# Where the exponentials of the next unit stand among ScalarE's copies in a multi-head attention loop

## What is computed

```
x = x + L0_xattn(ctx, ctx, layernorm(x))      # 16 heads, softmax((q k^T) / sqrt(128)), out @ W_out.T + b_out
x = x + L0_ffn(layernorm(x))                  # 8 experts, the best 2 weighted, gelu
x = x + L1_xattn(layernorm(x), ctx)           # 1 head
x = x + L1_ffn(layernorm(x))                  # 8 experts and a shared one
x = x + L2_xattn(layernorm(x), ctx)           # 16 heads, two softmaxes: attn1 - lambda * attn2, rms norm, projection
x = x + L2_ffn(layernorm(x))                  # 8 experts with a capacity
x = x + L3_xattn(layernorm(x), ctx)           # 16 heads, rotated q and k, a bias by position, a gate
x = x + L3_ffn(layernorm(x))                  # 8 experts, silu(a) * g
```

```
attn = softmax(q @ k.T * scale, axis=-1)      # 512 x 77 per head and batch
out = attn @ v                                # heads side by side, then a projection to 128
```

## Time and profile before

| | |
|---|---|
| median of 3 runs | 1227.28 us (1226.39 to 1229.32) |
| profiled execution, its own time | 1229.32 us |
| its span | 1227.5 us |
| PE busy | 975.9 us, 79% |
| PEld busy | 824.3 us, 67% |
| DVE busy | 636.9 us, 52% |
| ACT busy | 550.9 us, 45% |
| POOL busy | 398.7 us, 32% |
| mean granted TensorE clock | 0.87 |

### The profile page before, as it was taken

One profiled execution on the slowest core, in us unless ns is written; L12 is line 12 of the kernel. 1 busy time (PEld: TensorE's weight loads), 2 busy tenths in 40 slices (PEclk: granted clock), 3 DMA queues, 4 the chain that ended last, 5 costly groups with the idle time before them and its releaser, 6 DMA issues. The chain is left out here.

```text
span 1227.5 us, 20580 instructions
## 1 busy us (share of the span) xinstructions
PE 975.9 (79%) x7706; PEld 824.3 (67%) x7706; DVE 636.9 (52%) x1741; ACT 550.9 (45%) x1051; POOL 398.7 (32%) x396
## 2 busy tenths in 40 slices
PE   3887999999978999878888742989349876199992
PEld 3565899999957999745666522888226664188882
DVE  7787311111266343668788723344377784444442
ACT  1665444344434334346556421655327543155552
POOL 4443200000013002400010244446555546635551
PEclk9988899999996899979889755999769776589996
DMA  9999900000000000000000003655200000355543
GB/s 336 168 172 167 187 33 2 1 1 1 1 1 1 1 1 1 1 1 2 1 1 2 10 26 114 187 168 176 74 1 1 2 5 27 93 162 183 167 148 103
DMA packets 70577, 83.69 MB, mean 68 GB/s; under 512 B 5297, under 2 KB 57528, under 8 KB 70352
## 3 DMA queue, kind: packets, MB, share of 16 engines
q1 hardware_dynamic: 64336, 71.85, 25.9%
q0 software_dynamic: 4992, 8.45, 2.0%
q10 hardware_dynamic: 1152, 2.10, 0.5%
HBM read 52.02 MB, written 32.18 MB: 69 GB/s over the span
## 5 line engine op out<-in xcount | busy, mean ns | idle before, releaser
L2198 ACT ACTIVATE hT<-PS,par 128x512 f32<-128x512 f32 x200 | 136.8, 688 | 184.3 <-PE PS L2146 182.8
L2238 DVE SCALAR_TENSOR_TENSOR X<-PS,wts,X 128x128 f32<-128x128 f32 x272 | 76.6, 344 | 230.0 <-PE PS L2158 230.0
L822 PE MATMUL PS<-par,score 128*116 128x128 f32 x704 | 117.3, 308 | 18.9 <-ACT score L1035 6.2
L1054 ACT ACTIVATE hT<-PS 116x512 f32<-116x512 f32 (+1 forms) x192 | 102.1, 560 | 56.5 <-PE PS L822 55.2
L2158 PEld LDWEIGHTS PS<-regA,hT 128*128 128x128 f32 x1024 | 119.2, 192 | 2.8
L2158 PE MATMUL PS<-regA,hT 128*128 128x128 f32 x1024 | 119.4, 275 | 0.0
L822 PEld LDWEIGHTS PS<-par,score 128*116 128x116 f32 x704 | 90.4, 153 | 30.3 <-issue 16.3
L1123 POOL TENSOR_TENSOR score<-score,mx 128x1232 f32<-128x1232 f32 x32 | 72.0, 2251 | 101.3 <-DVE mx L931 101.3
L1909 PE MATMUL PS<-q_up,halves 128*112 128x256 f32 (+1 forms) x276 | 88.0, 319 | 15.3 <-DVE hT L2021 8.7
L835 PE MATMUL PS<-hT,vblk 116*32 116x128 f32 x1408 | 85.3, 302 | 10.4 <-DVE oc L951 9.5
L2144 PE MATMUL PS<-x_up,w_halves 128*128 128x512 f32 x200 | 88.0, 440 | 0.0
(11 more groups left out here) (304 smaller groups left out, 2033.7 us busy)
## 6 DMA issues: line engine op xcount, KB each, us to landing
regA<-L3f_w SPq DMA_DIRECT2D x23, 704.0 KB
regB<-L2f_w SPq DMA_DIRECT2D x23, 578.0 KB
L2f_sorted_x<-empty_row SPq DMA_DIRECT2D x8, 1161.0 KB, 22.2
L3f_sorted_x<-empty_row SPq DMA_DIRECT2D x8, 1161.0 KB, 21.7
regA<-L0f_w SPq DMA_DIRECT2D x4, 768.0 KB, 16.6
regA<-L2f_sorted_x SPq DMA_DIRECT2D x23, 129.0 KB, 3.7
regB<-L3f_sorted_x SPq DMA_DIRECT2D x23, 129.0 KB, 4.0
par<-params SPq DMA_DIRECT2D x1, 2386.0 KB, 13.4
```

What stands on the lines that cost most here:

```text
L822: last = nc.tensor.transpose(PS[0:BW, bank_of(("exps", 3 * u + i)), (j % 4) * P:(j % 4) * P + P], exps_of(u)[:, first:first + BW], ident)
L1054: nc.scalar.activation(hT[0:BW, u % 2, i, 0:width], PS[0:BW, bank, 0:width], ACT.Copy).then_inc(pT_ready.sem, 1)
L2198: nc.scalar.activation(hT[:, n % 2, k, :], PS[:, i % 4, :], c["act"], bias=pc(f"{tag}_b1")[:, col:col + 1]).then_inc(h_ready.sem, 1)
```

## The change

In ScalarE's program, `exps(u + 1)` goes from behind `evacuate_pT(u, 2)` to behind `evacuate_pT(u, 0)`. `evacuate_pT(u, 1)` goes behind the copy of the attended tile.

```diff
@@ -1069,17 +1069,16 @@
                         evacuate_oT(done)
                     if u < units:
                         evacuate_pT(u, 0)
-                        evacuate_pT(u, 1)
+                    if u + 1 < units:
+                        exps(u + 1)
                     if tag == "L3x" and done is not None:
                         evacuate_attT(done)
                     if u < units:
+                        evacuate_pT(u, 1)
                         g = route["logits_group"](u) if route else None
                         if g is not None:
                             route["scalar_rows"](a, g, bank_of(("rows", g)))
                         evacuate_pT(u, 2)
-                    if u + 1 < units:
-                        exps(u + 1)
-                    if u < units:
                         evacuate_sums(u)
```

## The result

| | before | after |
|---|---|---|
| median | 1228.30 us (4 runs, 1226.39 to 1232.22) | 1249.89 us (4 runs, 1249.63 to 1250.99) |
| ratio | | 1.0168, 95% interval 1.0141 to 1.0194 |
| profiled execution, its own time | 1229.32 us | 1237.48 us |
| span | 1227.5 us | 1235.7 us |

The change costs 20.6 us (0.0168 x 1228.3; 17 to 24 by the interval). The quotient of the two medians is 1.0176; the ratio in the table is the one on record, whose result lists 21 executions of the changed kernel, from 1237.48 to 1253.91 with a median of 1249.74. 1246 us had been forecast, in a range of 1236 to 1262. Two later sets of runs of the changed kernel gave 1.0145 (1.0114 to 1.0177) and 1.0156 (1.0134 to 1.0178), 18 to 19 us.

What follows compares the result with a forecast made beforehand. TensorE was taken as busiest, with the end of copy 2 already on its path. Layers 0, 2 and 3 add 5.8 + 6.4 + 6.4 = 18.6 us, giving 1246 us, 1.5% slower, range 1236 to 1262.

Steps and rivals of the forecast that it cites:

- A regular unit of layer 0, +0.60: Layer 0 attention: copy 2 ends 0.81 us later, the freed copy of the sums returns 0.21, so +0.60 us a unit.
- Layer 2, +0.60 and +0.22: Layer 2 attention: seven odd units pay 0.60 us, ten even or first ones 0.22, in all 6.4 us.
- Layer 3, +1.13: Layer 3 regular units: copy 2 ends at 2.91 instead of 1.78 us, +1.13 each, nothing comes back; layer total 6.4.
- Units 1 and 49, +1.8 each: Second units of layers 0 and 3: exponentials wait for GpSimd's shift, delaying copies 1 and 2; +1.78 and +1.79 us.
- Routing groups cost nothing and swallow the unit ahead: Layer 2 units 26, 34, 42: moved exponentials fall into ScalarE's idle time; these and the odd units ahead cost 0.
- VectorE's bursts in layer 0 take all but 0.2: Layer 0 units 6 to 8, 10 to 12: VectorE's normalisation absorbs all but 0.21 us per burst, 0.42 in all.
- Layer 3, units 60 to 63 pay nothing: End of layer 3's attention: these units wait for VectorE and GpSimd, so the change adds 0.
- The sum, 18.6: All three attention stages: 5.8 for layer 0, 6.4 for layer 2, 6.4 for layer 3, together 18.6 us slower.
- the clock (1): Rival 1, regular units: new idles cost TensorE its clock, 1.5 us a unit; 1262 to 1294, taken 1275 us; chance 0.08.
- Rival 2: Layers 3 and 0: late GpSimd shifts stall the exponentials in every unit, 7 to 10 us more, 1255 us; chance 0.08.
- Rival 3: All stages: TensorE's first matmuls and VectorE's slack hide the delay, only units 1 and 49 pay; 1230 us; chance 0.09.
- Rival 4: Some 27 units: freeing the copy of the sums wins 0.15 to 0.21 us each, 4 to 5 us; 1222; chance 0.05.

## Why the prediction was right, step by step

- *A regular unit of layer 0, +0.60.* Measured 5.08 - 4.49 = 0.59. The steps inside it are right too: last loads at 2.64, transposes of the sums at 3.82 (forecast 3.83).
- *Layer 2, +0.60 and +0.22.* Measured 4.97 - 4.38 = 0.59 behind odd units and 5.20 - 4.98 = 0.22 in even ones.
- *Layer 3, +1.13.* Measured about 1.05: behind the exponentials the attended tile's copy holds ScalarE for 0.25 (959.20 to 959.45), not 0.32.
- *Units 1 and 49, +1.8 each.* Mis-sized: 3.5 each. The stall for GpSimd was forecast, and right up to the last weight loads at 4.06; the clock that it costs, 1.7 us each, stood only in the bounds, as 3 to 5. The run without these units shows 7.4 us for both.
- *Routing groups cost nothing and swallow the unit ahead.* Right, and too small a gain: they keep their clock more often (layer 2's first: 8.3 to 8.4 in place of 10.0 to 10.8 us), and layer 2 costs 4.1 in place of 6.4. In layer 3 I had given 1.08 back; units 54 and 55 took 14.5 to 17.8 us with the new order against 19.1 before.
- *VectorE's bursts in layer 0 take all but 0.2.* Right where the clock was alike: units 10 to 12 took 18.93 to 18.94 us with the new order and 18.72 in two kernels with the old one (the change in layer 3 only, in the groups only), with a mean clock of 0.85 to 0.86 in all, so 0.21 more. For units 6 to 8 no such pair is there. Over the whole stage the term can't be read: kernels with the old order took 76.6, 77.8, 78.0, 80.4 and 82.8 us, with 3 to 14 us at half clock. With the new order it was 86.1 to 86.2 four times.
- *Layer 3, units 60 to 63 pay nothing.* Not decided: units 60 to 62 took 20.0 to 24.3 us in five profiles with the old order in them and 21.3 to 24.9 in five with the new one.
- *The sum, 18.6.* Measured 18 to 21. The errors of the terms went both ways: layer 0 cost 8.9 us where 5.8 had been forecast, layers 2 and 3 cost 4.1 and 3.9 where 6.4 had been forecast for each. The mechanism and the periods of the units are right by their own numbers; that the sum came so near is in part luck, as layer 0's 3.1 us above its forecast stand against 4.8 us below in the other two.

Of the rivals, the clock (1) came true at units 1 and 49 and failed in regular units. In layer 2, from 589 on, where each unit has an idle of 0.65 us for copy 1, the changed kernel held full clock:

```profile
589.00:605.00 16.00, 12.41 (x145) 8.09 (x146) 12.56 (x33) 10.15 (x18) 1.75 (x3) 1.00 0.01 2
```

By the rule of the Trainium skill that the prediction names (TensorE: Matmul & The Clock Gate, "A second HAM failure mode: psum-queue depth-cycling"), brief idles in every iteration could have made the clock swing here; this trace doesn't agree, as the matmuls' idles of 0.65 us (0.90 in units 51 to 53 of layer 3) came with 1.00.

The prediction's own test, that waits of over 2 us have a slow stretch near them and waits of one don't, is too simple. Before the change, matmuls of layer 0 waited 1.36 us at 93.99 and ran at 0.71 over the next 3 us; they waited 1.51 at 100.82 and ran at 1.00. Rival 2 is wrong: in regular units of layer 3 the exponentials start 0.49 behind copy 0 with no wait for GpSimd's shift, which is in step, as forecast. Rival 3 is wrong by the 5.08 us. Rival 4 is wrong too, since copies 1 and 2 had no room. With the sums' copy put first, their transposes in layer 0 start at 3.01 behind copy 0 instead of 3.23, so that wait was on the path, but TensorE then waits for the exponentials and the whole gains nothing.

No version here beat the kernel before: the two that didn't lose (routing groups only, sums first) are at 0.9994 and 1.0003, within their intervals of no change.

## What to carry to other kernels

In an in-order queue, put work for this unit ahead of work for the next, and ask of each instruction when its reader starts: the exponentials had 0.85 us of room, and the last copy had none (its reader starts 0.05 behind its end). What a long instruction delays is read from the last short one behind it; it doesn't matter how many are. And an instruction that itself waits for another engine is worst ahead of work whose data is there, as the idle that TensorE gets by it may also cost it its clock, here 1.7 us on top of 1.8.

## What the runs showed of the hardware

- A wait of 1.78 us in unit 1 came with a granted clock of 0.68 to 0.71 over the unit in all four profiles that have it, and a wait of 1.46 us there, with the exponentials behind copy 1, came with 0.70. But the length of an idle did not settle the clock by itself: in unit 34 of layer 2 the same wait of 1.16 us came with 1.00 in the first profile of the changed kernel and 0.67 in the second, and in unit 55 of layer 3 a wait of 1.65 us came with 0.63 in the first and one of 1.64 with 1.00 in the third.
- A kernel made slower in regular units was faster in the routing groups. In layer 2's first, the wait ahead of it fell from 1.75 to 1.16 us, the clock over the unit rose from 0.58 to 0.79, and the unit took 8.3 us instead of 10.8 (10.0 and 10.2 in two other profiles of the old order).
- While GpSimd issues scatters (0.96 us each), TensorE's signal for the copy of the sums came 1.1 to 5.5 us behind the modelled end of its last matmul, in ten of eleven profiles whose scatters stand in the attention. The stretch of four units took 30 to 34 us with it and 21 to 23 without.
- Stages whose instruction lists are equal differed by 6 us (76.6 to 82.8) between kernels, mostly by their stretches at half clock. A change of a few us wants the timed runs, and a change of a part of one wants the period of single units.
